# Half of the bidiagonal steps of a Mamba scan made by VectorE, one product per pair of states

## The reference

```
x_in, z = split(x @ in_proj_w.T + in_proj_b)       # 512 channels each
x_conv = silu(causal conv over 4 taps of x_in)
dt_low, Bm, Cm = split(x_conv @ x_proj_w.T)        # 64, 16 and 16
dt = softplus(dt_low @ dt_proj_w.T + dt_proj_b)
A_bar = exp(dt[..., None] * A)                     # 16 states a channel
h = A_bar * h + (A_bar - 1) / A * Bt * xt          # over time
y = sum over states of h * Ct + D * xt
out = (y * silu(z)) @ out_proj_w.T + out_proj_b
```

## Time and profile before

| | us |
|---|---|
| median of 3 executions | 2379.16 (2376.68 to 2380.75) |
| the profiled execution | 2379.85 |
| its span, first to last instruction | 2378.0 |
| TensorE busy | 2111.4 |
| VectorE busy | 1768.7 |
| ScalarE busy | 1835.2 |
| GpSimd busy | 1772.8 |
| ScalarE making steps (L662, 1024 instructions) | 255.9 |
| VectorE scanning (L1129, 1024) | 1281.5 |
| mean granted clock of TensorE | 0.963 of full |

### The profile page before, as it was taken

The page is one execution under the profiler, slowest core; times in us unless marked ns, Lnnn a source line. Parts: engine busy times, 40 slices in busy tenths (PEclk is TensorE's granted clock), DMA queues, the critical chain, the costliest instruction groups (busy, mean ns, idle before and its releaser), DMA issues. The chain is left out here.

```text
span 2378.0 us, 68478 instructions
## 1 busy us (share of the span) xinstructions
PE 2111.4 (89%) x26114; PEld 1270.0 (53%) x26114; DVE 1768.7 (74%) x2992; ACT 1835.2 (77%) x4074; POOL 1772.8 (75%) x1716
## 2 busy tenths in 40 slices
PE   6888989898989898989898989898989878899997
PEld 2454545454555554545455555555545544688864
DVE  2687878787878788787878787878786878555556
ACT  5787888888888879797979797978787875455537
POOL 2688787878686969696969787878787877476654
PEclk8899999999999999999999999999999999899999
DMA  2132333333333323333223232323222333796667
GB/s 92 55 95 89 103 90 95 98 93 93 96 94 93 99 89 96 93 91 92 91 83 99 75 113 79 104 89 100 92 91 93 89 108 98 229 278 213 197 195 265
DMA packets 159218, 269.19 MB, mean 113 GB/s; under 512 B 26536, under 2 KB 74284, under 8 KB 158510
## 3 DMA queue, kind: packets, MB, share of 16 engines
q1 hardware_dynamic: 143294, 220.01, 30.6%
q0 software_dynamic: 15600, 44.79, 5.4%
HBM read 206.27 MB, written 58.45 MB: 111 GB/s over the span
## 5 line engine op out<-in xcount | busy, mean ns | idle before, releaser
L574 POOL TENSOR_TENSOR hc<-h,c_rep 128x512 f32<-128x512 f32 x1024 | 1284.8, 1276 | 369.6 <-DVE h L1129 122.6
L1129 DVE TENSOR_TENSOR_SCAN h<-g_ps,carry,h 128x512 f32<-128x512 f32 x1024 | 1281.5, 1274 | 104.2 <-ACT h L646 79.8
L646 ACT ACTIVATE h<-dt,a_mat 128x512 f32<-128x512 f32 x1024 | 692.0, 712 | 17.4 <-POOL hc L574 16.4
L924 PEld LDWEIGHTS g_ps<-b_steps,x_conv_rows 64*64 64x64 f32 x16384 | 491.5, 137 | 331.4 <-issue 237.5
L924 PE MATMUL g_ps<-b_steps,x_conv_rows 64*64 64x128 f32 x16384 | 569.4, 278 | 74.2 <-DVE h L1129 67.8
L885 PE MATMUL y_ps<-hc,dg_inv 64*64 64x512 f32 x2048 | 525.3, 628 | 23.1 <-POOL hc L574 22.5
L886 PE MATMUL y_ps<-hc,dg_inv 64*64 64x512 f32 x2048 | 523.9, 628 | 0.0
L885 PEld LDWEIGHTS y_ps<-hc,dg_inv 64*64 64x64 f32 x2048 | 141.5, 139 | 261.3 <-issue 168.1
L662 ACT ACTIVATE b_steps<-steps_of,bc_tok 128x64 f32<-128x64 f32 x1024 | 255.9, 341 | 0.0
L1628 POOL DMA_INDIRECT y_planes<-gathered,home x144 | 138.5, 962 | 97.3 <-DVE gathered L2032 74.4
L1120 DVE TENSOR_TENSOR g_ps<-g_ps,minus_u 128x16 f32<-128x16 f32 x512 | 86.8, 170 | 129.8 <-PE g_ps L924 127.2
(11 more groups left out here) (277 smaller groups left out, 2893.1 us busy)
## 6 DMA issues: line engine op xcount, KB each, us to landing
c_rep<-bc_rows SPq DMA_DIRECT2D x512, 256.0 KB
gathered<-slot_rows SPq DMA_DIRECT2D x144, 129.5 KB
gathered<-y_planes SPq DMA_DIRECT2D x32, 512.0 KB, 7.7
x_t<-in_x_t SPq DMA_DIRECT2D x16, 512.0 KB, 3.6
x_tok<-in_x_tok SPq DMA_DIRECT2D x16, 512.0 KB, 4.1
out<-x_t SPq DMA_DIRECT2D x16, 512.0 KB, 2.9
x_t_rows<-y_gated SPq DMA_DIRECT2D x15, 512.0 KB, 3.0
x_t<-x_t_rows POOLq DMA_DIRECT2D x15, 512.0 KB, 5.2
```

The lines of the kernel that those rows point to most:

```text
L574: nc.gpsimd.tensor_tensor(hc[:, at_all % HCS], h[:, at_all % SLOTS], c_rep[:, at % CS], ALU.mult).then_inc(hc_ready, 1)
L646: nc.scalar.activation(h[:, (ITEMS * u + m) % SLOTS], dt[:, c], ACT.Exp, scale=a_mat[:, c, s:s + 1]).then_inc(factor_ready, 1)
L924: one = nc.tensor.matmul(g_ps[some, e, r * T + k * P:r * T + (k + 1) * P], x_rows[rows, c, k, some], steps_of, start=True, stop=True)
L1129: nc.vector.tensor_tensor_scan(slot, du, slot, carry[:, batch(u), c, s:s + 1], ALU.add, ALU.mult).then_inc(scanned, 1)
```

## The change

One line changes:

```diff
-BY_SCALAR = (0, 1, 2, 3, 4, 5, 6, 7)
+BY_SCALAR = (0, 1, 2, 3)
```

## The result

Five executions of the changed kernel took 2391.76 us in the median (2389.47 to 2393.59), five of the kernel before beside them 2380.08 (2376.68 to 2381.01): a ratio of 1.0050, 95% interval 1.0035 to 1.0064. It is slower, by 11.7 us. Its profiled execution has a span of 2390.1 us, 12.1 more than that of before.

A forecast was written before the change was run, and what follows sets the result against it. No engine alone bounds it: a loop of ScalarE, VectorE, then TensorE does. Terms -1.7 + 1.2 - 0.1 + 1.4 + 0.3 = +1.1 us a unit, 16.5 over 15 units, on 2379.2: 2396 us, range 2369 to 2410.

The forecast's parts named there:

- Pair 4 leaves ScalarE: ScalarE's order at 1039.73 loses 2.0 us, so factor h and the scan at 1051.73 come 1.7 us sooner: -1.7 a unit.
- the sign that its first step is wrong: In the changed kernel's profile: the biases come sooner but the scan at 1051.73 doesn't.
- Pair 4 on VectorE: Product behind scan 2, in VectorE's idle time at 1038.64: costs nothing, or 0.6 us if that cover were gone.
- the 1.27 us wait: VectorE's idle time for ScalarE at 1038.64, behind scan 2, taken to cover pair 4's product.
- A product's own time: Duration of one new 128x512 product on VectorE: taken as 0.6 us, bounds 0.6 and 1.28.
- Pairs 5 and 6: Two products behind scan 16, ahead of L1033, uncovered: +1.2 us a unit; their removal from ScalarE gives -0.1.
- a wait for GpSimd: Products behind scan 16 held until GpSimd's instruction ends: 0.2 us for the first, 1.2 for the second, +1.4 a unit.
- the prediction's first rival: Unheld products: VectorE and GpSimd don't meet, pairs 5 and 6 wait under 0.6 us; -0.6 a unit, 2370 us; chance 0.26.
- the sign of a hold: L1033 later by 2.6 us against the factor behind the sigmoid, by 1.2 if unheld.
- Pair 7: Product behind scan 26, at 1092.75, held by GpSimd's hc, so its fill is late: +0.3 us a unit.
- 15 units with the same cost: The projection exists in 15 units, each charged the same +1.1 us: 16.5 us in all.
- GpSimd becomes the bound: Rival: each product waits a whole hc, GpSimd comes 2.4 us late; +2.6 a unit, 2418 us; chance 0.12.

The follow-up runs named there:

- e1: Against the kernel before, only pair 4 moved to VectorE, behind scan 2: 2396.47 us, ratio 1.0006, unit 123.1 to 123.6.
- e2: Against the kernel before, only pairs 5 and 6 moved to VectorE, behind scan 16: 2492.33 us, ratio 1.0407, unit 129.7.
- e4: Against the kernel before, only pair 4 on VectorE, behind scan 50 of the unit before: 2385.30 us, ratio 0.9965.
- e8: Changed kernel (pairs 4 to 7 on VectorE) with pair 4 moved behind scan 50: 2450.80 us in one execution, the kernel before 2396.29.
- e7: Against the kernel before, pairs 0 and 4 on VectorE, both behind scan 50 of the unit before: 2404.66 us, ratio 1.0025.
- e6: Against the kernel before, only pair 4 on VectorE behind scan 2, as eight 128x64 instructions with a scalar column: 2433.39 us, ratio 1.0134.
- e9: Against the kernel before, only pairs 5 and 6 on VectorE, one scan earlier, behind scan 15: 2442.37 us, ratio 1.0177.

## Why the prediction was right

It said 2396 (2369 to 2410) and slower with 0.59; it is 2391.8. The unit was forecast at 124.0 and is 124.07. The direction and the kind of cost were right. That the number came out right is luck: two wrong terms cancel.

- *Pair 4 leaves ScalarE*, -1.7: right as the biases' gain (1.9). The rest of the step, that the scan at 1051.73 comes as much sooner, failed: it comes 0.13 us sooner. The prediction names this as the sign that its first step is wrong, and so it is.
- *Pair 4 on VectorE*, 0: wrong, and the largest error. I held the 1.27 us wait for its cover and bounded the uncovered case at 0.6. It is held to the end of the run of hc in 12 of the 15 units behind unit 0, 3.3 to 4.0 us, and eats the 1.7: with e1 the two terms together are +0.2, not -1.7.
- *A product's own time*, 0.6: right, 0.60 from start to start.
- *Pairs 5 and 6*, +1.2 - 0.1, and *a wait for GpSimd*, +1.4: together 2.5, measured 0.65 (L1033 is 0.85 late in the changed kernel and 0.20 in e1). Their own time is there, 4.90 us from the start of scan 16 to L1033 against 3.70 in e1; 0.55 of it comes back ahead of scan 16. They weren't held. I took the wait as at most one hc and as spread by chance. It is neither: it can be three hc and a scatter (e2: 5.3 us for the two), or nothing, by 0.65 us of alignment that repeats from unit to unit. The waits of the two are under the 0.6 us at which the prediction's first rival was to hold, and L1033 is 1.0 us later against the factor behind the sigmoid (3.19 less 2.20), not the 2.6 given as the sign of a hold but near the 1.2 of none.
- *Pair 7*, +0.3: right (0.25 alone).
- 15 units with the same cost: the first unit gained 5.7 us instead (102.56 us from its L695 to the next, before 108.26), and the second lost 2.3. In the trace of before the first unit's fill at 92.28 waited 3.52 us for ScalarE's steps; pair 4 alone (e1) gives 3.3 of the 5.7, pairs 5 and 6 alone (e2) 3.9. With 1.13 in each of the 15 units the whole would have been some 2397, an estimate.

An error of +1.9 for pair 4 and one of -1.85 for pairs 5 and 6 cancel. The mechanism was right in kind, that a product with its operands in SBUF can be held by GpSimd and that this takes away ScalarE's relief (unheld, e4 shows 1.5 to 1.9 us of it); where it bites and for how long was wrong. The Trainium skill, page "SBUF — State Buffer", section "Who interferes with whom", has the loser blocked for the whole of the other's instruction. The traces agree that it is blocked whole, and show that it can be so through several instructions in a row. The rival "GpSimd becomes the bound" had the right idea of pair 4 and of longer waits, but GpSimd, which it made 2.4 us late, lost half a microsecond (L542): it won.

Pairs 5 and 6 alone cost 97 us (e2), and all four with pair 4 elsewhere 54 (e8). The range didn't hold such cases and no rival had them.

## What to carry to other kernels

A VectorE instruction that works from SBUF to SBUF can cost, beside a busy GpSimd, not its duration but the time until GpSimd leaves a gap: place it where GpSimd waits (behind scan 50 here, 0.67 us) or just ahead of an instruction with issue time before it (the scatters here), not ahead of a run of large operations. Don't add up such costs from one-part experiments: each moves the alignment of the next, and the same two products cost 0.65 or 6.8 us a unit. And price a long stall of TensorE with the half-speed time behind it.

## What the runs showed of the hardware that I had not expected

- A held product can lose at each boundary of back-to-back hc (up to 4.9 us for a 0.6 us product), while a GpSimd operation held by VectorE waits for one product: the hc of e7 took 1.63 us instead of 1.27 and went ahead of VectorE's second product.
- In the run of five hc, a product that came within 0.08 us of the fourth one's start won the next boundary (5 of 5), one that came in the third not (25 of 25). Elsewhere two products won 0.55 and 1.03 us into an hc. I name no cause.
- VectorE's product with a scalar, with one input in SBUF, is held like the one with two (e6: 3.51 us instead of 0.25).
- Where TensorE's wait for the output projection's bank is 1.73 us, the granted clock stays at 2.4 GHz. Where it is 2.30 us (e9), the clock falls to 1.2 GHz just behind it, and where it is 5.80 us (e2), within it; the rest of the unit is then 1.6 to 1.7 us longer.
- A scatter, an indirect DMA that GpSimd issues, is held by the product as well: 1.46 us instead of 1.00 at 1065.73.
- Steady states with a period of more than one unit: e8 alternates between two units of 123.4 and two of about 131. In the short ones the first product comes 0.1 us into the hc ahead of the scatter, in the long ones 0.4 us into the scatter.
